# Two transformer layers on one core: the later keys of layer 1's attention split from a plain buffer, and its output projections moved

## What is computed

```python
q = einsum('bsh,he->bse', x, w_q).reshape(b, sq, GROUPS, HPG, KVC)     # 4 groups of 4 heads, 128 wide
k, v = split(einsum('bsh,he->bse', x, w_kv), 2, axis=-1)               # one key and value per group
scores = einsum('bqgpd,bkgd->bgqpk', q, k) * SCALE                      # causal mask, softmax
ctx = einsum('bgqpk,bkgd->bqgpd', probs, v).reshape(b, sq, HEADS * KVC)
out = einsum('bse,eh->bsh', ctx, w_dense)
```

## Time and profile before

| | us |
|---|---|
| three runs | 1456.45, 1463.96, 1448.93; median 1456.45 |
| the profiled execution | 1450.06, its span 1448.8 |
| around the span | 1.3 |
| PE busy in the span | 1294.8 (89%) |
| VectorE, ScalarE, GpSimd busy | 874.5, 780.0, 441.0 |
| chain that ended last, by engine | PE 69%, VectorE 11%, issue 6%, DMA 6%, ScalarE 4%, GpSimd 4% |

### The profile page before, as it was taken

One profiled execution on the slowest core, in us unless ns is written; L12 is line 12 of the kernel. 1 busy time (PEld: TensorE's weight loads), 2 busy tenths in 40 slices (PEclk: granted clock), 3 DMA queues, 4 the chain that ended last, 5 costly groups with the idle time before them and its releaser, 6 DMA issues.

```text
span 1448.8 us, 22556 instructions
## 1 busy us (share of the span) xinstructions
PE 1294.8 (89%) x6461; PEld 913.3 (63%) x6461; DVE 874.5 (60%) x2649; ACT 780.0 (54%) x1907; POOL 441.0 (30%) x577
## 2 busy tenths in 40 slices
PE   6689799887889998799999999999999986999994
PEld 5334344334556776577777777787777764678773
DVE  5678687753553365765577566666676754543555
ACT  3267575653431545566666556665566643166562
POOL 5344545220344644200000006001410140455553
PEclk9689898987989999899999999999999997999997
DMA  6653617003213553144200001000100018555664
GB/s 219 135 123 84 154 31 151 2 2 149 107 49 99 162 163 100 36 143 140 69 1 1 16 1 60 1 16 1 45 16 16 1 44 326 186 158 156 209 192 139
DMA packets 79207, 133.99 MB, mean 92 GB/s; under 512 B 13788, under 2 KB 52708, under 8 KB 77420
## 3 DMA queue, kind: packets, MB, share of 16 engines
q1 hardware_dynamic: 62128, 92.39, 20.8%
q0 software_dynamic: 15712, 38.25, 9.4%
q10 hardware_dynamic: 1248, 1.90, 0.4%
HBM read 77.20 MB, written 60.00 MB: 95 GB/s over the span
## 4 chain that ended last, share of the span: by engine, by line
PE 69%; DVE 11%; issue 6%; DMA 6%; ACT 4%; POOL 4%; DVEq 0%; SPq 0%; ACTq 0%; POOLq 0%
PE psum L126 9%; PE psum L1984 8%; PE psum L128 8%; PE psum L127 8%; PE psum L2628 7%; PE psum L2674 4%; PE psum L1955 4%; PE psum L2501 4%; PE psum L854 3%; PE psum L883 3%; PE psum L2535 2%; PE psum L2597 1%; PE psum L778 1%; DVE a_nmax L790 1%; POOL slots L1635 1%
## 5 line engine op out<-in xcount | busy, mean ns | idle before, releaser
L790 DVE TENSOR_REDUCE a_nmax<-psum 128x2 f32<-128x1024 f32 x128 | 155.1, 1217 | 66.5 <-PE psum L778 65.5
L869 ACT ACTIVATE a_et<-psum 128x512 f32<-128x512 f32 x256 | 139.0, 594 | 92.0 <-PE psum L854 88.5
L1930 ACT ACTIVATE a_spare<-psum,a_nmax 128x128 f32<-128x128 f32 (+3 forms) x256 | 134.7, 526 | 93.4 <-DVE a_nmax L1919 87.6
L1919 DVE CUSTOM_DVE_ANT_0 psum<-psum,a_spare 128x128 f32<-128x128 f32 (+3 forms) x256 | 126.7, 495 | 79.4 <-PE psum L128 78.6
L2697 POOL DMA_INDIRECT results<-r_fin,r_to x134 | 134.3, 1002 | 123.0 <-ACT r_fin L2689 63.1
L1984 PE MATMUL psum<-a_et,a_v 128*128 128x512 f32 (+3 forms) x512 | 169.5, 433 | 0.0
L2628 PE MATMUL psum<-m_w,m_xT 128*128 x536 | 150.5, 403 | 0.0
L1964 ACT ACTIVATE a_et<-psum 128x128 f32<-128x128 f32 (+3 forms) x256 | 111.6, 436 | 64.2 <-PE psum L1955 60.7
L126 PE MATMUL psum<-a_kT,a_q 128*128 128x128 f32 (+3 forms) x256 | 118.9, 465 | 6.8 <-DVE a_q L1858 5.9
L854 PE MATMUL psum<-a_stk 50*128 50x512 f32 x256 | 109.0, 500 | 15.0 <-ACT a_et L869 12.1
L1955 PE MATMUL psum<-ident,a_spare 128*128 128x128 f32 x640 | 113.5, 275 | 0.6 <-DVE a_spare L1943 0.6
(11 more groups left out here) (326 smaller groups left out, 2940.6 us busy)
## 6 DMA issues: line engine op xcount, KB each, us to landing
r_xs<-slots SPq DMA_DIRECT2D x134, 129.0 KB, 2.3
slots<-empty SPq DMA_DIRECT2D x12, 1290.0 KB, 6.6
m_w<-in_experts SPq DMA_DIRECT2D x16, 768.0 KB, 14.3
stacks<-a_qk SPq DMA_DIRECT2D x32, 256.0 KB, 3.8
a_stk<-stacks POOLq DMA_DIRECT2D x32, 256.0 KB, 7.0
r_shared_hid<-results SPq DMA_DIRECT2D x12, 512.0 KB, 4.6
m_w<-in_experts SPq DMA_DIRECT2D x4, 1216.0 KB, 14.2
a_stk<-stacks POOLq DMA_DIRECT2D x32, 128.0 KB, 6.3
```

Source lines behind the costliest of these rows:

```text
L790: dve.tensor_reduce(nmax[:, G % 2, qt, 2 * p:2 * p + 2], psum[:, n:n + 2, :], AX.X, ALU.max, negate=True).then_inc(s_max.sem, 1)
L869: act.activation(et[:, n % NET, 2 * p + hh, :], psum[:, 4 + hh, :], ACT.Exp).then_inc(s_e.sem, 1)
L1919: dve.tensor_tensor_reduce(psum[:, n, 0:W], psum[:, n, 0:W], mask[:, S - W:S], 1.0, BIG, ALU.add, ALU.min, nmax[:, u % NE, :]).then_inc(s_ ...
L1930: act.activation(e[:, u % NE, 0:W], psum[:, n, 0:W], ACT.Exp, bias=nmax[:, u % NE, :], scale=-1.0, accum_out=rsum[:, u % NE, :]).then_inc( ...
```

## The change

Batch 0's keys stay as they were. The keys of batches 1 to 3 now go another way. ScalarE copies the bank to a plain fp32 buffer k32 (`scalar_k32`), and the bank is free with that copy. One step later ScalarE copies k32 to the hi half (`scalar_k_hi`, after the exponential of that step), and GpSimd subtracts hi from k32 to give lo (`gpsimd_k_lo`). The buffer k32 is the second half of oT, so `scalar_k32` waits until oT has been turned, and `vector_out` waits until GpSimd has read k32.

The two halves of the output projection are issued at r = 5 and 7: the first at step 1 of the next head, the second at its step 3. `vector_out` goes from the start of VectorE's step 74 to the end of its step 75 (in `vector_late`, where the key's subtraction was). `tensor_back` stays at 77.

```diff
--- before.py
+++ after.py
@@ -1814,6 +1814,7 @@
             g.free[n] = first_free[n]
         e = weights.spare[:, 0:NE * S].rearrange("p (n s) -> p n s", s=S)
         oT = weights.spare[:, NE * S:NE * S + KT * S].rearrange("p (n s) -> p n s", s=S)
+        k32 = oT[:, KT - 1, :]
         mask = weights.spare[:, NE * S + KT * S:NE * S + KT * S + S]
         q = sb("q", [P, 2, 2, S], F32R)
         et = sb("et", [P, TT * (TT + 1), P])
@@ -1828,6 +1829,28 @@
         mask_in = s_mask.up(16)
 
 
+
+        s_k32, s_klo_p, k32_free = k.sem("act_k32"), k.sem("pool_k_lo"), [None]
+
+        def scalar_k32(b, i):
+            if k32_free[0]:
+                act.wait_ge(*k32_free[0])
+            if oT_free[0]:
+                act.wait_ge(*oT_free[0])
+            act.wait_ge(*kv_done[b, 0, i])
+            act.activation(k32[:, :], psum[:, kv_bank[b, 0, i], :], ACT.Copy).then_inc(s_k32.sem, 1)
+            g.free[kv_bank[b, 0, i]] = k_ready[b, i, "32"] = s_k32.up()
+
+        def scalar_k_hi(b, i):
+            act.wait_ge(*k_free[i])
+            act.wait_ge(*k_ready[b, i, "32"])
+            act.activation(kT[:, i, 0, :], k32[:, :], ACT.Copy).then_inc(s_khi.sem, 1)
+            k_ready[b, i, "hi"] = s_khi.up()
+
+        def gpsimd_k_lo(b, i):
+            pool.wait_ge(*k_ready[b, i, "hi"])
+            pool.tensor_tensor(kT[:, i, 1, :], k32[:, :], kT[:, i, 0, :], ALU.subtract).then_inc(s_klo_p.sem, 1)
+            k32_free[0] = k_ready[b, i] = s_klo_p.up()
 
         q_bank, q_done, q_ready = {}, {}, {}
         q_free = [None] * 2
@@ -2021,6 +2044,8 @@
         def vector_out(b):
             if oT_free[0]:
                 dve.wait_ge(*oT_free[0])
+            if k32_free[0]:
+                dve.wait_ge(*k32_free[0])
             dve.wait_ge(*o_done[b, H1 - 1])
             for m in range(KT):
                 dve.tensor_scalar(oT[:, m, :], psum[:, o_banks[m], :], k.gate[1][:, 0, m, b:b + 1], None,
@@ -2155,8 +2180,8 @@
                     if r == 2:
                         tensor_pv(b, h, 2)
                         tensor_pv(b, h, 3)
-                    if r in (4, 5):
-                        tensor_out(b, h, r - 4)
+                    if r in (5, 7):
+                        tensor_out(b, h, (r - 5) // 2)
                 if d in (77, 81):
                     tensor_back(b, (d - 77) // 4)
             if 0 <= s < B * U:
@@ -2173,8 +2198,6 @@
                 h, r = q_at(d - 1)
                 if r == KT - 1 and (b, h) not in q_ready:
                     vector_q(b, h)
-                if d == 74:
-                    vector_out(b)
                 if d in (77, 81):
                     vector_back(b, (d - 77) // 4)
             if 0 <= s - 1 < B * U:
@@ -2236,10 +2259,8 @@
         def vector_late(s):
 
             for b in range(B):
-                d = s - U * b
-                j = kv_at(d) if b else None
-                if j is not None and j < G1:
-                    vector_k(b, j)
+                if s - U * b == 75:
+                    vector_out(b)
 
         def scalar(s):
             w, d = batch_of(s)
@@ -2253,7 +2274,7 @@
                 d = s - U * b
                 j = kv_at(d) if b else None
                 if j is not None and j < G1:
-                    scalar_k(b, j)
+                    scalar_k32(b, j)
                 elif j is not None:
                     scalar_v(b, j - G1)
                 for h, r in out_at(d):
@@ -2266,6 +2287,10 @@
                 scalar_et(s - 2)
             if 0 <= s < B * U:
                 scalar_exp(s)
+            for b in range(1, B):
+                j = kv_at(s - U * b - 1)
+                if j is not None and j < G1:
+                    scalar_k_hi(b, j)
             w, d = batch_of(s)
             if d - 1 in NORM_AT and w + 1 < B:
                 norm.scalar_half_hi(w + 1, NORM_AT.index(d - 1))
@@ -2279,6 +2304,10 @@
 
         def gpsimd(s):
             w, d = batch_of(s)
+            for b in range(1, B):
+                j = kv_at(s - U * b - 1)
+                if j is not None and j < G1:
+                    gpsimd_k_lo(b, j)
             if d - 2 in NORM_AT and w + 1 < B:
                 norm.gpsimd_half_lo(w + 1, NORM_AT.index(d - 2))
             j, odd = divmod(s - DENSE_AT, 2)
```

## The result

The changed kernel takes 1441.42 us (median of 20 runs, 1435.71 to 1452.86), the kernel before, run beside it, 1456.82 (20 runs). Their ratio is 0.9904, with a 95% interval of 0.9884 to 0.9923: 1.0% less time. The forecast was 1449.0 us, 0.5% less, with 1434 to 1464 as its range. The direction was right, and the gain is about twice what I had summed up. The profiled execution of after took 1440.54 us, 9.5 less than that of before.

A forecast was written before the change was run, and what follows sets the result against it. Layer 1's attention was taken as bound by PE, busy 574.1 of 602 us. Terms: 15.3 - 3.1 + 0.8 - 2.0 + 3.5 - 1.3 - 5.7 = 7.5 us won, so 1456.45 - 7.5 = 1449.0 us; range 1434 to 1464.

The forecast's parts named there:

- 15.3 us at the keys: PE's 12 waits for a key's subtraction to free its bank, in layer 1's attention: all 15.3 us go.
- (a) the reloads: At three keys where ScalarE reloads its tables, PE waits for the exponential instead: 3.1 us lost, bounds 0 and 5.4.
- (b) the clock: After one key wait at a reload the clock fell to 0.72; half is counted, 0.8 us won, bounds 0 and 1.7.
- Blocked scalings: GpSimd's new key subtractions hold VectorE's scaling of step 2: 2.0 us lost, bounds 0 and 13.8.
- the scaling slips into the subtraction: At second and third keys of batches 2 and 3, VectorE's earlier side work delays the scaling: four cases, 0.5 us each.
- some 0.7 us of slack ahead of PE: Slack before PE needs a blocked scaling; it takes part of VectorE's 1.15 us delay, leaving 0.5 us each.
- ctx +3.5: PE's waits for ctx's lo half, 3.7 us, shrink to about 0.2 with projections moved: 3.5 us won, bounds 2.5 and 3.7.
- turnings -1.3: Step 3's later scores delay the maximum and `vector_q`, which frees the bank for turnings: 1.3 us lost, bounds 0 and 4.2.
- end of a batch -5.7: `tensor_back` waits behind GpSimd's subtraction, two multiplications and `vector_q`: 1.9 us in three batches, 5.7 lost, bounds 3.0 and 9.2.
- A: Batch ends are covered and no scaling is blocked: 17.6 us won, time 1438.9 us; chance 0.25.
- B: GpSimd's subtraction stops VectorE's scaling at all 12 keys, costing 13.8 us: 4.3 us lost, time 1460.8; chance 0.13.
- C: PE waits for step 3's scaling in every head, 0.4 us in some 60 heads: 24 us lost, time 1473.0; chance 0.14.

The follow-up runs named there:

- run 1: Against the changed kernel: projections back in steps 0 and 1, output scaling back at step 74, last key with its own k32 buffer; 1435.12 us, ratio 0.9921.
- run 5: Against the kernel with the changed keys alone: GpSimd's key subtraction two steps later, made to meet VectorE's scaling of the widest tile; 1442.76 us, ratio 0.9911.
- run 10: The changed kernel measured once more, with nothing changed against it; 1437.80 us, ratio 0.9936 to the kernel before.
- run 8: The kernel with the changed keys alone measured once more, with nothing changed against it; 1438.65 us, ratio 0.9863 to the kernel before.
- run 3: Against the changed kernel: each batch's last key uses two free buffers of the natural rows, not half the output buffer; 1432.57 us, ratio 0.9896.

## Why the prediction was right, and where its size was off

The mechanism was right: the waits for a key's bank went, and the chain at the end of a batch came link for link. The sum was 5 us short, and its parts show that it came as near as it did partly by luck.

- **15.3 us at the keys**: right, all gone with the keys alone. With the projections moved, 1.3 us come back as waits for the copy to k32, at the reloads.
- **(a) the reloads, 3.1 back**: 3.0 measured by pairs of heads (run 1). **(b) the clock, 0.8**: 1.2.
- **Blocked scalings, 2.0 back**: this term failed. In "the scaling slips into the subtraction: four cases" the mechanism is real (run 5), but the new subtraction lengthened none of 12 scalings, in two executions. Where VectorE had side work ahead of the scaling (at the third keys), the scaling still began 0.27 us ahead of the subtraction, against 0.36 in a plain head. And "some 0.7 us of slack ahead of PE" left a price of 0.2 to 0.4 us a stop at step 3's scaling (run 5) in place of 0.5; at step 2's, the one that was meant, a stop of 0.85 us cost the first head of run 10 0.8. Moreover the nine other keys gave 0.7 us more than PE had waited.
- Together the keys: forecast 11.0, measured 15.2 and 13.6 (runs 1 and 8 against the one trace of before); up to the last maximum, without the tail, 14.4 and 13.1.
- **ctx +3.5, turnings -1.3, end of a batch -5.7**: together -3.5; measured -2.6 (596.7 against 594.1) and -3.1 (598.8 against 595.7). The end of a batch cost 5.0 us of waits in place of 5.7, by the chain that was written down link for link; with GpSimd out of it 3.6 (run 3). The other two were both undervalued, and the errors cancel, which is luck. Against run 1 the turnings wait 5.1 us more (6.9 against 1.8), not 1.3. At ctx the waits fell by 5.6 us (7.2 to 1.6), and PE's busy time by another 3.5, which most likely belongs there too.
- **Rivals.** A (no returns, 17.6) has the nearer median for a wrong reason: no scaling is blocked by the new subtraction, but the returns at the ends of batches did come; by the stage, 12.6 lies half way between it and the forecast. B is out because none of the 12 was blocked. Its price of 13.8 us is not refuted: the 3 to 4 us of run 5 are for step 3's scaling, and the stops of step 2's in run 10 cost nearly their own length. C is out: a plain head still takes 7.92 us.

So the missing 5 us of the stage (12.6 against 7.5) are 2.0 for the blocking that didn't come, 0.5 at reloads and clock, 0.7 at keys that gained more than their wait, 0.8 in the tail, 0.2 at other heads, and 0.9 at the projections. This splits one pair of traces, which repeat within 2.1 us.

The second part of the change won nothing: the keys alone are at least as good, and projections alone are slower than before. What it gave back, 2.6 to 3.1 us, is 1.6 for the buffer shared with the output (run 3) and about 1 for the moved projections, which is inside the scatter.

## What to carry to other kernels

Judge a change part by part: here one part won 14 to 15 us, and the other gave some 3 back with the buffer that it shared, hidden inside a sum that looked fine. An eviction that frees a PSUM bank should be one operation, with the rest of the work where no queue holds anything urgent behind it; with the same subtraction at the same place of VectorE's queue the stage is 17 us longer than before and not 15 shorter. Moving work of PE one step later pays where the next wait is the one it covers, and only by place: cut the trace by period and compare place by place before moving it everywhere.

## What was not expected of the hardware

- GpSimd's subtraction of 128x512 held a scaling of VectorE from SBUF that met it for 0.8 to 1.3 us (12 of 12 in run 5), whether the subtraction came 0.15 to 0.27 us ahead of it or 0.19 and 0.22 us behind it, and was not lengthened itself (1.27 to 1.30 us). Two such subtractions in a row held one scaling for both: 3.01 us in run 10, begun 0.28 us ahead of them. But 12 scalings of the changed kernel, begun 0.27 to 0.38 us ahead, kept their 0.42 us; where the limit lies these rows don't say. The maximum from PSUM beside the same subtraction took 0.69 to 0.70 us.
- PE's busy time is not the same for the same matmuls: at a clock of 1.00 it was 563.3 us with the projections early and 559.7 with them late, where weight loads waited 14.5 and 3.0 us for ctx. That the first holds waits of weight loads is likely, not shown.
- A chance meeting of a GpSimd copy, timed by a DMA, with one VectorE instruction held it for 0.7 us; PE waited 1.43 us there in one execution and not at all in another of the same kernel. The other half of that wait has no cause in the rows.
